# Attention by head pairs in the two 64-row halves of the array, and value halves regrouped by DMA

## What is computed

```python
x = x + attention(layernorm(x))
x = x + ffn(layernorm(x))

# attention, per sequence and head; scale = 64 ** -0.5
xn  = rms_norm(x, gamma)
q, k, v = split(xn @ w_qkv)              # 16 heads of 64
sim = (q * scale) @ k.T                  # 512 x 512
out = softmax(sim) @ v                   # 512 x 64
y   = concat(out) @ w_out

# ffn
top = top_k(softmax(x @ router_w), 2);  combine = top / sum(top)
y   = (gelu(x @ w1 + b1) @ w2 + b2) * sum(combine)
```

## Time and profile before

| | us |
|---|---|
| median of 3 runs | 1307.66 |
| lowest and highest | 1306.78, 1311.88 |
| span of the profiled execution | 1307.2 |
| attention (first to last unit), about | 22 to 1085 |
| feed-forward stage, about | 1085 to 1307 |
| TensorE, VectorE, ScalarE, GpSimd busy, whole span | 98%, 81%, 69%, 42% |

### The profile page before, as it was taken

The page is one execution under the profiler, slowest core; times in us unless marked ns, Lnnn a source line. Parts: engine busy times, 40 slices in busy tenths (PEclk is TensorE's granted clock), DMA queues, the critical chain, the costliest instruction groups (busy, mean ns, idle before and its releaser), DMA issues.

```text
span 1307.2 us, 22347 instructions
## 1 busy us (share of the span) xinstructions
PE 1278.9 (98%) x7748; PEld 1114.1 (85%) x7748; DVE 1052.8 (81%) x1930; ACT 905.1 (69%) x1989; POOL 551.2 (42%) x732
## 2 busy tenths in 40 slices
PE   5899999999999999999999999999999999999998
PEld 4688888888888888888888888888888887888887
DVE  6799888988898889888988898889888985666554
ACT  4688777777777777777777777777777786333432
POOL 2245444444444444444444444444444456322321
PEclk9999999999999999999999999999999999999999
DMA  6455444544454445444544454445444541101100
GB/s 184 106 123 136 88 96 95 143 92 98 97 145 98 97 98 146 97 97 98 139 104 95 95 123 106 92 96 124 108 94 95 124 113 54 65 33 41 57 17 33
DMA packets 41629, 128.80 MB, mean 99 GB/s; under 512 B 7664, under 2 KB 9968, under 8 KB 41520
## 3 DMA queue, kind: packets, MB, share of 16 engines
q1 hardware_dynamic: 41520, 127.38, 41.8%
HBM read 19.08 MB, written 8.39 MB: 21 GB/s over the span
## 4 chain that ended last, share of the span: by engine, by line
PE 91%; DVE 2%; POOL 2%; ACT 2%; DMA 1%; issue 1%; SPq 1%; DVEq 0%; ACTq 0%; POOLq 0%
PE ps L415 39%; PE ps L460 17%; PE ps L446 16%; PE ps L437 8%; PE ps L436 8%; DMA stack<-nat 1%; DVE pT_lo L811 1%; DMA wstage<-in_w_qkv 1%; ACT prob L680 1%; PE ps L483 1%; PE ps L540 0%; POOL prob L724 0%; PE ps L529 0%; POOL wbig_lo L750 0%; DVE negmax L879 0%
## 5 line engine op out<-in xcount | busy, mean ns | idle before, releaser
L724 POOL TENSOR_SCALAR prob<-prob,rowinv 128x512 f32<-128x512 f32 x512 | 348.9, 694 | 580.9 <-DVE rowinv L884 580.8
L680 ACT ACTIVATE prob<-ps,negmax 128x512 f32<-128x512 f32 x512 | 348.7, 693 | 6.0 <-DVE negmax L879 2.5
L811 DVE TENSOR_TENSOR pT_lo<-ps,pT_hi 128x512 fp32r<-128x512 f32 x512 | 327.7, 681 | 23.6 <-ACT pT_hi L654 23.6
L879 DVE TENSOR_REDUCE negmax<-ps 128x2 f32<-128x1024 f32 x256 | 311.9, 1218 | 29.5 <-PE ps L437 26.4
L654 ACT ACTIVATE pT_hi<-ps 128x512 fp32r<-128x512 f32 x512 | 278.4, 600 | 55.9 <-PE ps L446 55.4
L446 PE MATMUL ps<-identity,prob 128*128 128x128 f32 x2048 | 266.8, 273 | 2.2 <-POOL prob L724 2.0
L446 PEld LDWEIGHTS ps<-identity,prob 128*128 128x128 f32 x2048 | 234.9, 140 | 22.5 <-POOL prob L724 4.3
L437 PE MATMUL ps<-stack 128*128 128x512 f32 x508 | 200.4, 395 | 0.0
L436 PE MATMUL ps<-stack 128*128 128x512 f32 x508 | 199.0, 392 | 0.1
L460 PE MATMUL ps<-pT_lo,vbuf 128*128 128x512 f32 x512 | 150.7, 416 | 0.0
L460 PE MATMUL ps<-pT_hi,vbuf 128*128 128x512 f32 x512 | 150.3, 415 | 0.1
(11 more groups left out here) (109 smaller groups left out, 2204.5 us busy)
## 6 DMA issues: line engine op xcount, KB each, us to landing
stack<-nat SPq DMA_DIRECT2D x127, 384.0 KB, 3.9
stack<-nat SPq DMA_DIRECT2D x127, 256.0 KB, 4.9
stack<-nat SPq DMA_DIRECT2D x127, 128.0 KB, 4.9
xin<-in_x SPq DMA_DIRECT2D x8, 512.0 KB, 4.8
xres<-in_x SPq DMA_DIRECT2D x8, 512.0 KB, 3.4
x_scratch<-xres SPq DMA_DIRECT2D x8, 512.0 KB, 2.8
out_y<-f_o SPq DMA_DIRECT2D x16, 256.0 KB, 2.0
prob<-in_w_qkv SPq DMA_DIRECT2D x5, 512.0 KB, 4.9
```

The costliest lines, as they stand in the source:

```text
L680: act.activation(prob[:, n % NPROB, j * SEQ:(j + 1) * SEQ], ps[:, PS_SCORE[n % 2] + j, :], ACT.Exp, bias=negmax[:, n % 4, j:j + 1], accum_ ...
L724: return pool.tensor_scalar(dst, src, scalar, 1.0, ALU.mult, ALU.mult)
L811: return dve.tensor_tensor(dst, full, hi, ALU.subtract)
L879: dve.tensor_reduce(negmax[:, n % 4, :], ps[:, PS_SCORE[n % 2]:PS_SCORE[n % 2] + 2, :], AX.X, ALU.max, negate=True).then_inc(s_max, 1)
```

## The change

The unit becomes one tile of 128 queries of a pair of heads, so that the two score banks of a unit hold two heads and not two query tiles. Two units `2s` and `2s + 1` are one step, and every engine's loop is now over steps.

- **Scores.** There is no `stack` and no DMA for it. q and k are read from `nat`, which has two buffers. The head at partitions 0 to 63 and the one at 64 to 127 are multiplied in turn, each over 64 rows and into its own bank, three partial products each: six matmuls of 512 columns a unit.
- **Transposes.** A unit's probabilities are transposed in blocks of 64 queries by 128 keys, 16 a unit, in turn from partitions 0 to 63 and from 64 to 127, into two banks: 4 and 5 for odd units, 6 and 7 for even ones. Bank 5 is also that of the weighted values, and banks 4, 6 and 7 those of the other blocks, which have two places in a step.
- **Weighted values.** The columns of v hi and v lo change sides from the even head of a pair to the odd one. A step has 16 matmuls of 256 columns for two heads and 256 queries. ScalarE copies the whole bank into `halves_out`. When both halves of the queries of a pair are there, four DMAs from SP (128 KB each, `regroup`) bring the v hi part of both heads into `att_hi_v` and the v lo part into `att_lo_v`, and GpSimd adds the two. VectorE's addition is gone.
- **Order.** A step on TensorE is: transposes of `2s - 3`, scores of `2s` and `2s + 1`, transposes of `2s - 2`, a first block of other work, the weighted values, the rest of the other work.

```diff
-        nat = sb("nat", [P, 4, SEQ], F32R)
+        nat = sb("nat", [P, 2, 4, SEQ], F32R)
-        stack = sb("stack", [P, NSTACK, 3, SEQ], F32R, att)
-        vlo_part = sb("vlo_part", [DH, SEQ], F32, att)
-        att32 = sb("att32", [P, SEQ], F32, att)
+        halves_out = sb("halves_out", [P, 2, 2, SEQ], F32, att)
+        att_hi_v = sb("att_hi_v", [P, SEQ], F32, att)
+        att_lo_v = sb("att_lo_v", [P, SEQ], F32, att)
...
+            def regroup(pair):
+                src = halves_out[:, pair % 2]
+                sp.wait_ge(s_halves, 2 * pair + 2)
+                if pair >= 1:
+                    sp.wait_ge(s_att, pair)
+                sp.dma_start(att_hi_v[0:DH, :], src[0:DH, 0, :]).then_inc(s_merge, 16)
+                sp.dma_start(att_hi_v[DH:P, :], src[DH:P, 1, :]).then_inc(s_merge, 16)
+                sp.dma_start(att_lo_v[0:DH, :], src[DH:P, 0, :]).then_inc(s_merge, 16)
+                sp.dma_start(att_lo_v[DH:P, :], src[0:DH, 1, :]).then_inc(s_merge, 16)
...
             def scores(n):
-                    pe.matmul(dst, stack[:, i, 0, q0:q0 + P], stack[:, i, 1, :], start=True, stop=False)
-                    ins = pe.matmul(dst, stack[:, i, 0, q0:q0 + P], stack[:, i, 2, :], start=False, stop=True)
+                for q_part, k_part in ((QH, KH), (QL, KH)):
+                    for h in range(2):
+                        rows = slice(h * DH, (h + 1) * DH)
+                        pe.matmul(ps[:, PS_SCORE[n % 2] + h, :], part[rows, q_part, q0:q0 + P], part[rows, k_part, :],
+                                  start=q_part == QH, stop=False)
+                for h in range(2):
+                    rows = slice(h * DH, (h + 1) * DH)
+                    pe.matmul(ps[:, PS_SCORE[n % 2] + h, :], part[rows, QH, q0:q0 + P], part[rows, KL, :],
+                              start=False, stop=True).then_inc(s_score, 1)
...
             def transpose_prob(n):
+                bank = PS_PT_ODD if n % 2 else PS_PT_EVEN
+                for a in range(2 * TT):
+                    for r in range(2):
+                        rows = slice(r * DH, (r + 1) * DH)
+                        ins = pe.transpose(ps[:, bank + r, a * DH:(a + 1) * DH],
+                                           prob[rows, n % NPROB, a * P:(a + 1) * P], identity[rows, rows])
...
+            def weighted_values(t):
+                pe.wait_ge(s_ptlo, 4 * t + 4)
+                for h in range(2):
+                    for part in range(2):
+                        for k in range(TT):
+                            ins = pe.matmul(ps[:, PS_OUT, h * 2 * P:(h + 1) * 2 * P],
+                                            vbuf[:, quad % 2, k, pair % 2 * 2 + h, :],
+                                            pT[part][:, t % 2, h * TT + k, :], start=part == 0 and k == 0,
+                                            stop=part == 1 and k == TT - 1)
+                ins.then_inc(s_pv, 1)
...
+            def copy_halves(t):
+                pair, part = divmod(t, 2)
+                act.wait_ge(s_pv, t + 1)
+                if part == 0 and pair >= 2:
+                    act.wait_ge(s_merge, 64 * (pair - 1))
+                act.activation(halves_out[:, pair % 2, :, part * 2 * P:(part + 1) * 2 * P],
+                               ps[:, PS_OUT, :].rearrange("p (h q) -> p h q", h=2), ACT.Copy).then_inc(s_halves, 1)
...
+            def attention_out(pair):
+                pool.wait_ge(s_merge, 64 * (pair + 1))
+                pool.tensor_tensor(att_hi_v[:, :], att_hi_v[:, :], att_lo_v[:, :], ALU.add).then_inc(s_head, 1)
+                times(attT[0][:, pair % NATT, :], att_hi_v[:, :], 1.0).then_inc(s_atthi, 1)
+                pool.tensor_tensor(attT[1][:, pair % NATT, :], att_hi_v[:, :], attT[0][:, pair % NATT, :],
+                                   ALU.subtract).then_inc(s_att, 1)
+
+            for step in range(FIRST_STEP, LAST_STEP + 1):
+                if 0 <= 2 * step - 1 < NUNIT:
+                    normalise_prob(2 * step - 1)
+                if step % 2 == 0 and 0 <= step // 2 - 2 < NPAIR:
+                    attention_out(step // 2 - 2)
+                if 0 <= 2 * step < NUNIT:
+                    normalise_prob(2 * step)
...
-                    dve.tensor_tensor(att32[head % 2 * DH:(head % 2 + 1) * DH, :], ps[0:DH, PS_OUT, :],
-                                      vlo_part[:, :], ALU.add).then_inc(s_head, 1)
```

More of the change, by code:

```diff
@@ new lines, in plan_aux @@
+    plan, index, place_of = {}, {}, []
+    for step in range(FIRST_STEP, LAST_STEP + 1):
+        b, rel = divmod(step, SPB_STEPS)
+        blocks = []
+        if step == -4:
+            blocks += [(1, "xt", 0, 0), (2, "xt", 0, 1)]
+        if step == -3:
+            blocks += [(1, "q", 0), (2, "k", 0)]
+        if step % 2 == 0 and step // 2 + 1 in range(1, NPAIR):
+            blocks += [(1, "q", step // 2 + 1), (2, "k", step // 2 + 1)]
+        if step % 4 == 3 and (step + 1) // 4 in range(NPAIR // 2):
+            blocks.append((1, "v", (step + 1) // 4, 0))
+        if step % 4 == 1 and step // 4 in range(NPAIR // 2):
+            blocks.append((1, "v", step // 4, 1))
+        if rel == 13 and 0 <= b < B:
+            blocks += [(2, "xt", b + 1, 0), (3, "xt", b + 1, 1)]
+        for half in range(2 * B - 1):
+            since = step - (8 * half + 11)
+            places = {0: 2, 2: 2, 4: 2, 6: 2} if half % 2 else {0: 2, 3: 3, 4: 2, 6: 2}
+            if since in places:
+                blocks.append((places[since], "out", half, list(places).index(since)))
+        for place, *task in sorted(blocks):
+            index[tuple(task)] = len(index)
+            place_of.append(place)
+            plan.setdefault(step, []).append((index[tuple(task)], place, *task))
@@ L241, in layer_kernel @@
         s_aux = sem("aux_block_done")
-        s_stack = [sem(f"head_stacked{i}") for i in range(NSTACK)]
         s_x1 = sem("x1_stored")
@@ new lines, in scores @@
+                q0 = tile * P
+                part = nat[:, pair % 2]
+                for q_part, k_part in ((QH, KH), (QL, KH)):
[7 more added lines that the diff above has]
+                              start=False, stop=True).then_inc(s_score, 1)
```

440 lines of the change are left out of this document (219 added, 221 removed).

## The result

The changed kernel takes 1262.54 us (four runs, 1262.11 to 1262.74); the kernel before took 1309.55 beside it (four runs, 1306.78 to 1311.88). The ratio is 0.9635 with a 95% interval of 0.9615 to 0.9656: 3.65% faster, where the forecast was 1323 us, 1.2% slower than its reference of 1307.66. The time lies in the range of 1200 to 1400, and the direction was wrong.

A forecast was written before the change was run, and what follows sets the result against it. TensorE was taken to bound the attention. Per step, -0.40 + 0.17 + 0.08 + 0.31 = +0.16 us, over 128 steps +20.5; 1307.2 + 20.5 - 4.65 = 1323 us, range 1200 to 1400.

The forecast's parts named there:

- What bounds the kernel: In the attention, TensorE's instruction list sets the time until another engine's loop is longer; 8.26 us per step before.
- Scores: TensorE, per step: six pairs of 64-row matmuls side by side at 0.24 us, 1.44 for 1.84, a gain of 0.40.
- Transposes: TensorE, per step: 32 half-array transposes at 0.061 us each, 1.95 for 1.78, a loss of 0.17.
- rival B: TensorE: weight loads of both halves overlap too; -0.87 us a step, 1191 to 1242 us; chance 0.34.
- Weighted values: TensorE, per step: sixteen 256-column matmuls at 0.12 us, 1.92 for 1.84, a loss of 0.08.
- the change of shape: TensorE, per step: switching from 128 to 64 rows and back once, a loss of 0.31 us.
- Start: TensorE's one long wait, for `nat` while `stack` was filled, goes: a gain of 4.65 us.
- End: Last pair's values pass through DMAs before the last output blocks: nothing counted, up to 4 us left in the range.
- Off TensorE: VectorE busy some 87 us less; VectorE and ScalarE loop of 7.2 us hidden under TensorE's 8.42 us step.
- D: GpSimd's wait for the regrouping DMAs decides once landing takes 5.5 us; 1355 to 1387 us; chance 0.13.
- C: TensorE: the halves don't run side by side, score pairs 0.48 us; 1507 to 1593 us; chance 0.10.
- The likeliest case: The forecast case: on TensorE the halves' streaming overlaps but not their weight loads; 1323 us, chance 0.43.

The follow-up runs named there:

- first experiment: Changed kernel with each unit's sixteen transposes ordered as eight from partitions 0 to 63, then eight from 64 to 127, instead of in turn: 1302.1 us.
- the small matmul: Changed kernel with one added 64-column matmul per step ahead of the weighted values: 1297.34 us over 64 rows, 1272.07 us over 128 rows (control).
- the last experiment: Changed kernel with VectorE's even-slot side tasks (layer norm) at its step's end, and v's last two weight chunks split one step earlier: 1246.13 us.
- its experiment: Changed kernel with VectorE's side tasks of an even slot, above all the next sequence's layer norm, moved to the end of its step: 1248.88 us.

## Why the prediction was wrong, point by point

**What bounds the kernel** was read rightly: before, TensorE's list was the time, and the part of the change to that list decided the sign.

**Scores**, 1.44 forecast, 1.48 measured: right. The pair costs 0.233 us, and the two of a pair start 0.03 apart.

**Transposes**, 1.95 forecast, 0.98 measured: this is the step that failed. The prediction gave bounds of 0.98 and 2.62 and took 0.061 for each, "for the halves may hide each other's streaming, but every block still loads 128 columns of weights". The price of one in a half is just 0.061 (first experiment), so the row was read well. What was wrong was the sentence that loads of the two halves come one after the other. It rested on no row, and the scores' term couldn't tell, since two loads of 0.12 fit under a 512-column matmul anyway. Sized at 0.98, the prediction's own sum is +0.16 - 0.97 = -0.81 a step, and the list measured is 7.47 - 8.26 = -0.79.

That is rival B, with a chance of 0.34. The rule that the Trainium skill ("TensorEngine Tiling (Array Packing)", Key Properties) has for it, that different tiles load and multiply in parallel, held, with 0.031 us for each load and transpose. The rule that was set against it (the Trainium skill, "TensorE: Matmul & The Clock Gate", the section on 56 against 53.3 ns: some 62 ns of sequencer for each matmul) is given there for hardware decoding off; how it is set here no run shows, but no such price binds in these rows, at 0.031. Its agreement with 0.061 was a coincidence, as the prediction had warned itself: the time of a load explained the row too.

**Weighted values**, 1.92 forecast, 1.90 measured, and **the change of shape**, 0.31 forecast, about 0.31 in the step and 0.26 by the small matmul: right. The latter is worth a look, since it was derived from two rows around four narrow transposes, and it is 0.31 x 128 = 40 us of the kernel. In the kernel before with half-array transposes it came to 0.34.

**Start**, 4.65 us forecast as a gain: it came out 4.6 later. The wait for `nat` is gone, but the order around it is another, and TensorE now waits 4.12 us for the split of v's weights. The prediction looked at what goes and not at what is late next. Behind that wait the clock is at 1.2 GHz, which costs another 1.3 us before the first scores (2.84 us for 1.57, by the last experiment); of the clock in the first steps the prediction said nothing. **End**, nothing forecast: 7.3 us more. One idle time of 2.74 us there is shown above. By windows from the last scores to the end, TensorE is busy 4.3 us longer (219.22 for 214.89) and idle 3.0 longer (10.19 for 7.23). The longer busy time has two sources that the rows show: twelve more 256-column matmuls of the output projection stand behind the last scores (72 for 60, 1.4 us), and 3.4 us of it are at 1.2 GHz, where the kernel before is at full clock. No experiment was made on either.

**Off TensorE.** VectorE lost 83 us where 87 were forecast. The loop was put at 7.2 us; measured, it holds every second step at 7.71. The sum missed that transposes of the next step need VectorE's lo part of the first block, behind a reciprocal and a maximum. It cost nothing at 8.42, and matters at 7.47. In B the prediction still said "above the 7.2 loop" and counted nothing for it.

**Why B's 1191 us were not reached.** B charged the loss to GpSimd (51 us, to 1242). The sign of that was right, the engine wrong: moving the regrouping brought nothing. Against B's 1191 the profiled span of 1260.8 is 70 us longer, and by the rows it adds up like this: 10 are the list (7.47 a step where B had 7.39), 36 the waits in the eight sequences (4.5 each), 6 the first ten steps, 9 the start and 7 the end, 68 in all. Of the 36, the layer norm ahead of the maximum is 8 or 9 (7.6 in seven sequences, by its experiment) and VectorE's lo part ahead of the transposes up to 0.24 us in every second step; the rest was not taken apart by experiments. In the last three terms the clock at 1.2 GHz has a part.

**D** was absent (landing 2.3 to 2.4 us); **C** too (a pair 0.23, not 0.48).

**The chances.** 0.34 and 0.43 for two cases that differ in a single assumption without a row, 0.8 us a step apart, shows how little was known. The likeliest case was the one in which only the streaming is side by side and not the loads; no row spoke for that over the other, so the sign was a coin's toss, and the forecast should have said so in its own number too.

## What to carry to other kernels

Where work of 64 rows or fewer exists for both halves of the array, put the two halves in turn, in small groups, and next to other work of 64 rows: side by side a load and a transpose of 64 x 64 cost 0.031 us instead of 0.061, while each change to 128 rows and back costs 0.26 to 0.31. If two cases of a forecast differ only in whether two things overlap, treat the sign as open, and price the gain by both. Once the bounding engine gets 10% shorter, ask of every other engine which of its instructions the first one waits for by then, and move what nobody waits for, such as a layer norm for later, behind it. Before an odd step is put down to the order of work, read the granted clock over it: a step in which the engine never stopped and that is long all the same was, here, a step at the lower clock.

## What the runs showed of the hardware that was not expected

- TensorE starts matmuls of one half of the rows ahead of earlier ones of the other half: three matmuls of 512 columns of one head and then three of the other ran in pairs 0.03 us apart. With transposes it reached three ahead: in groups of 4 and 4 nearly nothing was lost (1267.43 us, 1262.54 for alternating ones), with 8 and 8 the time was 1302.1.
- Weight loads of the two halves overlap: 0.031 us for each of 16 fp32 transposes of 64 x 64 with its load of 128 columns, 0.061 where all are in one half.
- A change between 128 and 64 rows isn't free: 0.26 us there and back around a single small matmul.
- TensorE's granted clock was at its lower level (1.2 GHz) for 23.9 us of the changed kernel's span and for 3.4 of that of the kernel before, behind stretches in which it had been idle for much of the time. The same step without any wait took 9.77 us at a clock of 0.74, 9.01 at 0.81 and 7.50 at 1.00.
